# Inverse roots for groups of four tiles in the output stage of a two-layer graph network

## The reference, cut to what matters

```python
edge_index = jnp.stack([src, dst])
x = _layernorm(x + _L0_gnn_ref(x, edge_index, ...), axis=-1)
x = _layernorm(x + _L1_gnn_ref(x, edge_attr_64, edge_index, ...), axis=-1)
return x
...
def _layernorm(x, axis=-1, eps=1e-05):
    m = jnp.mean(x, axis=axis, keepdims=True)
    v = jnp.var(x, axis=axis, keepdims=True)
    return (x - m) / jnp.sqrt(v + eps)
...
# the end of _L1_gnn_ref: sum of the messages of each destination, a gate between it and a skip path
out = jax.ops.segment_sum(msg, dst, num_segments=n).reshape(n, D_MSG)
x_r = m @ Wskip.T + bskip
beta = jax.nn.sigmoid(jnp.concatenate([out, x_r, out - x_r], axis=-1) @ Wbeta.T)
out = beta * x_r + (1.0 - beta) * out
return out @ W_m2n.T
```

## Time and profile before

| | |
|---|---|
| Median of three runs | 1283.99 us |
| The profiled execution | 1281.43 us |
| Its span, first to last instruction | 1279.6 us |
| Mean granted TensorE clock | 0.977 |
| PE busy | 1173.7 us, 92% |
| PEld busy | 1022.5 us, 80% |
| DVE busy | 1044.6 us, 82% |
| ACT busy | 828.8 us, 65% |
| POOL busy | 859.4 us, 67% |
| DMA | 276.99 MB, mean 216 GB/s |

### The profile page before, as it was taken

One profiled execution on the slowest core, in us unless ns is written; L12 is line 12 of the kernel. 1 busy time (PEld: TensorE's weight loads), 2 busy tenths in 40 slices (PEclk: granted clock), 3 DMA queues, 4 the chain that ended last, 5 costly groups with the idle time before them and its releaser, 6 DMA issues.

```text
span 1279.6 us, 28379 instructions
## 1 busy us (share of the span) xinstructions
PE 1173.7 (92%) x6982; PEld 1022.5 (80%) x6982; DVE 1044.6 (82%) x3794; ACT 828.8 (65%) x2783; POOL 859.4 (67%) x1074
## 2 busy tenths in 40 slices
PE   4699999999998699999999799999999995799995
PEld 3688998999897478878888589999999994678884
DVE  3477777777778889999999799999999986789885
ACT  0366666666566866666666756656666668589996
POOL 4688888888883355555554567777777754288888
PEclk9899999999999899999999999999999998799998
DMA  6658888888884388878887677767767743356662
GB/s 173 210 185 276 272 262 265 268 269 264 271 257 150 96 271 260 253 253 251 258 250 243 201 239 217 221 205 220 233 202 219 226 146 110 120 180 189 186 192 94
DMA packets 208795, 276.99 MB, mean 216 GB/s; under 512 B 40044, under 2 KB 140419, under 8 KB 208633
## 3 DMA queue, kind: packets, MB, share of 16 engines
q1 hardware_dynamic: 188793, 224.13, 55.6%
q0 software_dynamic: 19264, 50.85, 13.1%
q10 hardware_dynamic: 576, 0.20, 0.1%
HBM read 159.67 MB, written 117.12 MB: 216 GB/s over the span
## 4 chain that ended last, share of the span: by engine, by line
PE 59%; DVE 15%; issue 12%; POOL 7%; ACT 3%; DMA 1%; another core or an unknown queue 1%; DVEq 0%; SPq 0%; POOLq 0%; ACTq 0%
PE banks L744 20%; PE banks L857 7%; PE banks L734 6%; PE banks L1385 5%; POOL out L1538 4%; PE banks L847 3%; PE banks L1220 3%; POOL output_r L1544 3%; DVE AT L1246 3%; PE banks L859 3%; PE banks L1372 2%; PE banks L1390 2%; PE banks L1213 2%; PE banks L946 2%; PE banks L1370 2%
## 5 line engine op out<-in xcount | busy, mean ns | idle before, releaser
L744 PE MATMUL banks<-m_ext,node_XT 128*128 128x257 f32 x1568 | 376.6, 383 | 0.0
L744 PEld LDWEIGHTS banks<-m_ext,node_XT 128*128 128x128 f32 x1568 | 284.9, 192 | 33.1
L770 DVE SCALAR_TENSOR_TENSOR node_X<-banks,node_be,node_X 128x256 f32<-128x256 f32 x392 | 169.8, 475 | 81.7 <-ACT node_be L696 53.0
L671 POOL TENSOR_TENSOR node_r<-node_vv,half 128x4 f32<-128x4 f32 (+1 forms) x202 | 213.8, 1058 | 17.2 <-POOL node_vv L666 0.3
L702 ACT ACTIVATE node_XT<-banks 128x512 f32<-128x512 f32 x196 | 117.3, 599 | 131.2 <-PE banks L734 123.5
L666 POOL TENSOR_SCALAR node_vv<-node_mv 128x4 f32<-128x4 f32 (+1 forms) x202 | 59.4, 294 | 191.9 <-DVE node_mv L778 172.6
L709 ACT ACTIVATE node_sq<-node_X 128x256 f32<-128x256 f32 x392 | 157.8, 408 | 0.0
L683 ACT ACTIVATE node_X<-node_X,node_r 128x256 f32<-128x256 f32 x326 | 146.0, 497 | 1.4 <-POOL node_r L671 1.4
L763 DVE BATCH_NORM_STATS2 node_st<-node_X 128x6 f32<-128x256 f32 x392 | 145.6, 414 | 1.3 <-issue 0.5
L734 PE MATMUL banks<-ident,node_X 128*128 128x128 f32 x784 | 122.4, 279 | 19.3 <-issue 10.8
L824 POOL DMA_INDIRECT ring<-in_x,src_col x100 | 107.0, 1070 | 34.1 <-issue 14.1
(11 more groups left out here) (265 smaller groups left out, 2743.7 us busy)
## 6 DMA issues: line engine op xcount, KB each, us to landing
node_X<-in_x SPq DMA_DIRECT2D x196, 256.0 KB
out<-node_X SPq DMA_DIRECT2D x196, 256.0 KB
ring<-rows SPq DMA_DIRECT2D x210, 128.0 KB
rows<-ring SPq DMA_DIRECT2D x100, 256.0 KB
rows<-ring SPq DMA_DIRECT2D x200, 128.0 KB
MB<-keeps SPq DMA_DIRECT2D x40, 320.0 KB, 4.7
store<-rows SPq DMA_DIRECT2D x90, 128.0 KB
MB<-picks SPq DMA_DIRECT2D x50, 128.0 KB
```

Source lines behind the costliest of these rows:

```text
L671: pool.tensor_tensor(r[:, s % 4, NT * lo:NT * hi], v, self.c.half[:, NT * lo:NT * hi], ALU.pow).then_inc(self.roots, 1)
L744: last = pe.matmul(ps[:, NT * o + k, 0:D + 1], self.XT[:, o, k * D + h * P:k * D + (h + 1) * P], c.m_ext[:, h, :], start=(h == 0), stop=(h ...
L770: last = dve.scalar_tensor_tensor(out=X[:, n % U, k, :], in0=ps[:, b + k, 0:D], scalar=self.be[:, n % 4, k:k + 1], in1=X[:, n % U, k, :], ...
```

## The change

One tuple is changed. After two groups of one tile come 23 groups of four instead of 48 of two, and at the end three groups of two. All tables of steps and the sizes of the three small tiles (variances, roots, exponents, two columns to four) follow from it.

```diff
--- before.py
+++ after.py
@@ -1472,7 +1472,7 @@
         return emit
 
 
-GROUPS = (1, 1) + (2,) * 48 + (1, 1)
+GROUPS = (1, 1) + (4,) * 23 + (2,) * 3
 GROUP_AT = [sum(GROUPS[:g]) for g in range(len(GROUPS) + 1)]
 GROUP_OF = [g for g, size in enumerate(GROUPS) for _ in range(size)]
 WIDENED_AT, ROOTS_AT, SCALED_AT, SCATTERED_AT = {}, {}, {}, {}
```

## The result

The change made the kernel slower: 1308.18 us, the median of four runs (1306.21 to 1313.91), beside 1284.05 before, the median of four. The ratio is 1.0194, with a 95% interval of 1.0161 to 1.0227. The forecast was 1284.4 us, its range 1281.0 to 1287.2.

The account below looks back on a forecast made before the run. The prediction took TensorE's own pace, 1.64 us a tile, to bound the output stage, with GpSimd in a tie. Its terms, 0 (a, b) - 1.0 (c) + 1.46 (d) = +0.46 us, gave 1284.4 us, range 1281.0 to 1287.2.

Parts of the forecast that it names:

- (a): Roots of four in the output stage: GpSimd's work for four tiles falls from 6.52 to 6.14 us; effect on time 0.
- (b): Longer hold of a group in the output stage: ScalarE waits some 0.1 us a group for roots; cost nothing.
- (c): GpSimd's one pause of 1.74 us at 1136 us, output stage: new idle time mostly catches it up, -1.0 us.
- rival D: GpSimd's pause comes again and is not caught up: 1285.4 us, or 1287.2 behind the body's last root; chance 0.07.
- (d): End of the output stage: groups of four leave GpSimd more scatters behind the body's last roots, +1.46 us.
- B: GpSimd was the output stage's limit all along: 1276.0 us, with half of it 1280.8; chance 0.13.
- C: Output-stage loop of root, scale, third scatter, next root decides from roots of 2.01 us: 1288.4 us, slower; chance 0.10.

## Why the prediction was wrong

Point by point, in its own order.

(a) failed, and with it the sum. The step reads that GpSimd's work for four tiles becomes 6.14 us, that "none of it shortens the steady stage", and that TensorE "becomes the only limit". The prices were right: the root measured 1.042 us where I took 1.07 (two more values cost 0.29 us), and a scatter behind a scatter 0.30 + 0.98. What failed is that I priced a row of four scatters by its own durations alone, as if GpSimd's order could not reach TensorE. The experiment with two and with four in a row shows that it can: 30.8 us (1316.44 - 1285.60) for nothing but the order. The term that I set to 0 measures 18.1 us between tiles 10 and 90, 0.226 a tile.

(b) was right on what it looked at. ScalarE's wait for roots fell as forecast, and holding rows longer costs nothing, as the kernel with late scatters in twos shows. Its sentence that gate and copy "come in time" failed for another reason: they wait for TensorE's signals, not for a root.

(c) was wrong: the pause came again, 1.92 us, so there was nothing to recover. That was rival D; beside the rest its us or two can't be told apart. The pause stands ahead of the scatter of tile 13 in both kernels, and in eight of the nine others here too (0.74 to 2.78 us): it goes with a place in the program, which the prediction's one trace could not tell. What makes it stays open.

(d) was right in its own working, 17.18 us for 17.19 from the last four-wide root to the end, eleven scatters with no gap above 0.31. The root stood 1.4 us later behind TensorE's last transposes than I took, because the signals were late there too: the scan ahead of its addition starts at 1286.12, 1.41 us after its transpose's recorded end.

None of the rivals named the mechanism. B, GpSimd as the limit, falls: GpSimd's share went from 84.94 to 65.44 and the stage grew. Nor did the shares of the earlier trace rows name GpSimd, as the prediction reads them: ScalarE (90.55) and VectorE (89.92) stand above it. C needed roots of 2 us and they take 1.04. My range of 1281.0 to 1287.2 was made of bounds on durations, and had no place for an instruction that costs others more than itself.

The trace of before held the clue, in a stage that I had not opened. In the part `Score` GpSimd issues four gathers in a row. The timeline there, of GpSimd, TensorE and ScalarE:

```profile
261.49 1.10 POOL L824 DMA_INDIRECT ring<-in_x,src_col  x1 [0.19 <-issue]
262.90 0.95 POOL L824 DMA_INDIRECT ring<-in_x,dst_col  x1 [0.31 <-issue]
264.16 0.95 POOL L824 DMA_INDIRECT ring<-in_x,src_col  x1 [0.30 <-issue]
...
264.85 0.60 PE L847 MATMUL banks<-ident,ring 128*128 128x128 f32 x4
...
265.41 0.94 POOL L824 DMA_INDIRECT ring<-in_x,dst_col  x1 [0.30 <-issue]
...
267.21 0.60 ACT L870 ACTIVATE ST<-banks 128x512 f32<-128x512 f32 x1 [1.72 <-remote]
```

ScalarE's copy waits for four transposes that the trace lets end at 265.45, and starts 1.76 us later, 0.86 behind the fourth gather. In that kernel late signals over 0.7 us stand at 14 of 24 such rows of four gathers and at none of its rows of two. The wait is put to "remote", and TensorE has other work there, so it draws no eye.

A row alone is not enough, though. At the start of the same kernel GpSimd issues 18 gathers in a row, 0.30 us apart, from 14.48 to 37.02 us. In the timeline around the ninth, ScalarE's copy starts 0.04 us after the recorded end of the transposes that it waits for:

```profile
24.39 1.11 PE L847 MATMUL banks<-ident,ring 128*128 128x128 f32 x4
...
24.72 0.95 POOL L824 DMA_INDIRECT ring<-in_x,src_col  x1 [0.30 <-issue]
...
25.54 0.60 ACT L870 ACTIVATE ST<-banks 128x512 f32<-128x512 f32 x1 [19.63 <-issue]
```

Two more readers, at 24.50 and 27.41, are as prompt. TensorE was busy for 11.66 of 23.50 us there, and for 92 to 100 of 100 us in the output stage. Whether that is the difference, and why 10 of the 24 rows of four gathers show no signal that late, no run here tells.

## What to carry to other kernels

Before putting GpSimd's DMAs closer together, look in the trace at hand for a place where they already stand three or four in a row, and read how long after a matmul's recorded end its reader starts there. A wait on a matmul that has long ended, seen by two engines at once, points to late signals and not to TensorE's work; then it helps to spread the DMAs, and here 0.6 us of other GpSimd work after every second one sufficed. A row that is harmless in one stage, as the 18 gathers here, says nothing for another stage. Work taken off an engine that ties with the limit can have set the spacing of what that engine issues, so ask what the new spacing does as well as what the saved time is worth.

## What the runs showed of the hardware

- In the output stage, rows of three or four indirect DMAs on GpSimd, each 0.97 to 1.04 us with 0.30 to 0.46 between, hold TensorE's finished signals back by up to 1.40 us (three) and 2.44 (four; 2.55 with a quarter of the bytes); then several arrive within 0.1 us. In `Score` 14 of 24 rows of four did, and a row of 18 beside a half idle TensorE did not. Two in a row, with a root of 0.75 us between the pairs, do not (at most 0.52). VectorE's scan itself takes as long as in the kernels without late signals (478 ns mean in the kernel after, 480 with late scatters in twos).
- 0.13 us of other work after the second does not relieve it, 0.60 us does, and so does a pause of 1.27. Where the first groups' scatters stood 0.50 and 0.66 us apart, ahead of 1126 us in the kernel after, the signals were in time; that is one row.
- A quarter of the bytes changes neither the issue time nor the delay.

What in GpSimd's issue does this stays open. So does whether the matmuls themselves end late or only their signals, since the trace models their ends. The Trainium skill ("Perfetto Trace Analysis", section "Tensor Engine Instruction (MATMUL, LD_WEIGHTS)") says that TensorE's recorded end is an estimate from the instruction's size and not an observed end, and that the signal goes out only once the written data is acknowledged; the trace agrees in so far as the signals stand up to 2.55 us behind these ends. GpSimd DMAs other than scatters were not varied.
